# First mixture of an eight-expert layer: head statistics on VectorE and ScalarE, additions that leave sums, one of eight masked copies on GpSimd

## The reference, cut to what matters

```
y = scan output of the first branch                      # already computed, still unnormed
x = x + ga * (((y - mean(y)) * rsqrt(var(y) + eps)) * gamma + beta)
h = layernorm(x) * (1 + cb) + sb                         # per token, 128 features
sel = argmax(h @ gate_w + gate_b)                        # one expert of eight per token
x = x + gb * (h @ expert_w[sel] + expert_b[sel])
statistics of the new x                                  # for the next stage's layernorm
```

## Time and profile before

| what | us |
|---|---|
| median of 3 runs | 953.69 (953.1 to 953.91) |
| profiled execution: span, which is its own time here | 954.5 |
| TensorE busy in the span | 833.9 (87%) |
| VectorE busy | 776.2 (81%) |
| ScalarE busy | 656.3 (69%) |
| GpSimd busy | 568.8 (60%) |

### The profile page before, as it was taken

The page is one execution under the profiler, slowest core; times in us unless marked ns, Lnnn a source line. Parts: engine busy times, 40 slices in busy tenths (PEclk is TensorE's granted clock), DMA queues, the critical chain, the costliest instruction groups (busy, mean ns, idle before and its releaser), DMA issues.

```text
span 954.5 us, 23396 instructions
## 1 busy us (share of the span) xinstructions
PE 833.9 (87%) x7407; PEld 645.1 (68%) x7422; DVE 776.2 (81%) x2086; ACT 656.3 (69%) x1731; POOL 568.8 (60%) x571
## 2 busy tenths in 40 slices
PE   6969891699999957999999999999838999999990
PEld 5945471354445426888888888888617889999980
DVE  3988787889998858678999999999886866666996
ACT  3567126899996356567777877766456888888880
POOL 1211006757875143533688888888877777766773
PEclk9999796599999978999999999999858999999996
DMA  5330261322323203000011111111117666766987
GB/s 153 94 94 1 69 199 59 104 101 106 145 90 110 113 11 82 1 2 10 24 38 39 40 38 35 39 35 44 44 46 214 209 207 185 219 191 187 347 251 247
DMA packets 83461, 100.78 MB, mean 106 GB/s; under 512 B 15326, under 2 KB 65305, under 8 KB 81164
## 3 DMA queue, kind: packets, MB, share of 16 engines
q1 hardware_dynamic: 71388, 79.61, 27.3%
q0 software_dynamic: 8640, 17.97, 5.3%
q10 hardware_dynamic: 3312, 1.70, 0.6%
HBM read 75.71 MB, written 23.54 MB: 104 GB/s over the span
## 4 chain that ended last, share of the span: by engine, by line
PE 54%; DVE 4%; issue 2%; DMA 1%; SPq 1%; ACT 1%; POOL 0%; ACTq 0%; DVEq 0%
PE ps L2608 13%; PE ps L2365 12%; PE ps L2631 7%; PE ps L2381 3%; PE ps L2443 2%; PE ps L2356 2%; PE ps L2591 2%; PE ps L2327 2%; PE ps L2376 2%; PE ps L2502 2%; PE ps L2482 2%; PE ps L2342 1%; PE ps L2430 1%; PE ps L2626 1%; PE ps L2455 1%
## 5 line engine op out<-in xcount | busy, mean ns | idle before, releaser
L1551 POOL TENSOR_TENSOR kvb<-qk,v 128x1024 f32<-128x1024 f32 x64 | 126.2, 1976 | 74.6 <-DVE qk L1922 50.4
L1560 POOL DMA_INDIRECT rows_of<-payb,posu x128 | 144.7, 1131 | 40.7 <-issue 26.7
L1115 PE MATMUL ps<-masked,ew 128*128 128x512 f32 x256 | 129.9, 622 | 4.2 <-DVE masked L1043 3.5
L2365 PE MATMUL ps<-con,kvb 128*128 128x128 f32 x1024 | 126.0, 276 | 0.0
L2365 PEld LDWEIGHTS ps<-con,kvb 128*128 128x128 f32 x1024 | 119.4, 192 | 1.0 <-issue 1.0
L2287 DVE TENSOR_SCALAR qk<-ps,b 128x256 f32<-128x256 f32 x142 | 62.1, 479 | 47.7 <-PE ps L2608 43.2
L1043 DVE TENSOR_TENSOR masked<-f_t,wide 128x512 f32<-128x512 f32 x128 | 88.7, 711 | 9.6 <-PE ps L1115 9.3
L1584 POOL DMA_INDIRECT parts<-h,dest x72 | 76.9, 1068 | 26.6 <-issue 20.4
L1898 DVE TENSOR_TENSOR qc<-ps,qk 128x1024 f32<-128x1024 f32 x64 | 78.1, 1220 | 18.0 <-PE ps L2365 17.4
L1584 POOL DMA_INDIRECT parts<-gx,dest x70 | 75.4, 1077 | 25.5 <-issue 20.0
L1115 PEld LDWEIGHTS ps<-masked,ew 128*128 128x128 f32 x256 | 43.3, 193 | 47.2 <-issue 23.6
(11 more groups left out here) (367 smaller groups left out, 2130.4 us busy)
## 6 DMA issues: line engine op xcount, KB each, us to landing
wide<-hot_dram SPq DMA_DIRECT2D x16, 1024.0 KB, 4.6
kvb<-rows_of SPq DMA_DIRECT2D x71, 132.0 KB, 2.7
ex<-in_w_dram SPq DMA_DIRECT2D x36, 256.0 KB
lg<-in_w_dram SPq DMA_DIRECT2D x35, 256.0 KB
toep<-taps_dram SPq DMA_DIRECT2D x16, 512.0 KB, 5.8
xg<-parts SPq DMA_DIRECT2D x16, 512.0 KB, 5.5
x_tok<-in_x_dram SPq DMA_DIRECT2D x16, 256.0 KB, 3.0
rows<-rows_dram SPq DMA_DIRECT2D x16, 192.0 KB, 3.2
```

The costliest lines, as they stand in the source:

```text
L1115: nc.tensor.matmul(ps[:, w % 2, :], ew0[:, e, :], masked[e % 4][:, :], start=False, stop=(e == E - 1)).then_inc(s["product"], 1)
L1551: nc.gpsimd.tensor_tensor(kv[g % KB][:, :, :].rearrange("p e (h d) -> p e h d", h=H), k_in, v_in, ALU.mult).then_inc(s["kv"], 1)
L1560: nc.gpsimd.indirect_dma_start(rows_of, bass.IndirectOffsetOnAxis(ap=posu[w % PR][:, slot, t:t + 1], axis=0), pay[w % PB][:, t, :], None). ...
L2365: last = nc.tensor.matmul(cum(g)[:, e, :], kv[g % KB][:, e, :], k("upto"), start=True, stop=True)
```

## The change

VectorE and ScalarE make the statistics of the first four sequences alone: `statistics` for y for all sixteen, for x of sequences 0 to 3 `stats_x` (bn_stats and bn_aggr), the inverse root on ScalarE as Ln and Exp (`root_y`, `root_x`, with a table set loaded once), and `shift_x_head` on VectorE. For these sequences gamma is applied to (y - mean) in four pieces and the scale in `joined`, also four pieces. For sequences 4 to 15 `joined`, and for all sixteen `added`, are four scalar_tensor_tensor operations with a sum output in place of one addition and one reduction. `squares_y`, `sum_features`, `sum_x1` and `sum_x2` are gone. Mask 5 of every sequence and `bias_pieces` move to GpSimd. All five lists are written anew. The core of the diff:

```diff
-            moments = sb("moments", [P, 6 * C, 2], scope=sc)
+            moments = sb("moments", [P, TILES, 2], scope=sc)
+            HEAD = 4
...
+            BY_POOL = 5
             def expert(eng, name, w, e):
                 w, e = w + e // E, e % E
-                if exists(w):
+                if exists(w) and name == "masked":
+                    if e == BY_POOL:
+                        eng.wait_ge(s["masked_pool"], w + 1)
+                    else:
+                        eng.wait_ge(s["masked"], w * (E - 1) + e + (e < BY_POOL))
+                elif exists(w):
                     eng.wait_ge(s[name], w * E + e + 1)
...
-                    load_ahead(0)
-                    load_ahead(1)
-                    for w in range(B):
-                        load_ahead(w + 2)
-                        kept(w)
-                        spread(w)
+                    load_ahead(0); load_ahead(1); load_ahead(2); kept(0); spread(0); load_ahead(3); kept(1); spread(1); load_ahead(4)
+                    kept(2); spread(2); kept(3); spread(3); load_ahead(5); load_ahead(6); kept(4); spread(4); load_ahead(7); kept(5)
...
+                    def mask(w, e):
+                        landed(pool, s_wide, w)
+                        done(pool, "feat", w)
+                        expert(pool, "product", w, e - 4)
+                        nc.gpsimd.tensor_tensor(masked[e % 4][:, :], f_t[w % W][:, :], wide[w % W][:, e, :], ALU.mult).then_inc(s["masked_pool"], 1)
+
+                    nc.gpsimd.memset(eps[:, :], EPS).then_inc(s["eps"], 1)
+                    nc.gpsimd.tensor_scalar(down[:, :], k("iota"), -1.0, float(E), ALU.mult, ALU.add).then_inc(s["down"], 1)
+                    beta(0); beta(1); bias_pieces(); beta(2); beta(3); beta(4); beta(5); beta(6); beta(7); moments_mean(4); moments_scale(4)
+                    mask(0, 5); mean_x(4); mask(1, 5); beta(8); mean_2(0); scale_x(4); scale_2(0); moments_mean(5); moments_scale(5)
+                    moments_mean(6); moments_scale(6); moments_mean(7); moments_scale(7); moments_mean(8); moments_scale(8); mask(2, 5)
...
+                    def root(w, found, source, rs, logged, made):
+                        done(act, found, w)
+                        if w == 0:
+                            act.wait_ge(s["eps"], 1)
+                        nc.scalar.activation(tiles(rs, w), source[:, w * C:(w + 1) * C, 1], ACT.Ln, bias=eps[:, :]).then_inc(s[logged], 1)
+                        done(act, logged, w)
+                        nc.scalar.activation(tiles(rs, w), tiles(rs, w), ACT.Exp, scale=-0.5).then_inc(s[made], 1)
...
+                    nc.scalar.preload_act_table_set("natural_log_exp_and_others")
+                    root_y(0); root_y(1); root_x(0); norm_x(0); root_x(1); feat(0); root_y(2); norm_x(1); feat(1); hot_half(0); root_x(2)
...
+                    def stats_x(w):
+                        done(dve, "joined", w)
+                        done(dve, "stats_x", w - 1)
+                        for c in range(C):
+                            last = nc.vector.bn_stats(halves_x[:, c, :], x_tok[:, w * C + c, :])
+                        last.then_inc(s["sum_x"], 1)
+                        done(dve, "sum_x", w)
+                        for c in range(C):
+                            last = nc.vector.bn_aggr(moments_x[:, w * C + c, :], halves_x[:, c, :])
+                        last.then_inc(s["stats_x"], 1)
...
                     def gamma(w):
-                        if exists(w):
+                        if w < HEAD:
...
+                                last = nc.vector.scalar_tensor_tensor(yn[w % 2][:, c, :], features_of(t), moments[:, t, 0:1], rows[w % W][:, 0, :], ALU.subtract, ALU.mult)
...
-                            nc.vector.tensor_tensor(tiles(x_tok, w), tiles(x_tok, w), yn[w % 2][:, :, :], ALU.add).then_inc(s["joined"], 1)
...
+                                for c in range(C):
+                                    t = w * C + c
+                                    last = nc.vector.scalar_tensor_tensor(x_tok[:, t, :], yn[w % 2][:, c, :], rs_y[:, t:t + 1], x_tok[:, t, :], ALU.mult, ALU.add)
+                            else:
+                                for c in range(C):
+                                    t = w * C + c
+                                    last = nc.vector.scalar_tensor_tensor(x_tok[:, t, :], x_tok[:, t, :], 1.0, yn[w % 2][:, c, :], ALU.mult, ALU.add,
+                                                                          accum_out=sum_x[:, t:t + 1])
+                            last.then_inc(s["joined"], 1)
...
-                            nc.vector.tensor_tensor(tiles(x_tok, w), tiles(x_tok, w), ps[:, BACK, :].rearrange("p (c d) -> p c d", c=C), ALU.add).then_inc(s["added"], 1)
-
-                    def sum_x2(w):
-                        if exists(w):
-                            done(dve, "added", w)
-                            nc.vector.tensor_reduce(tiles(sum_2, w), tiles(x_tok, w), AX.X, ALU.add, negate=True).then_inc(s["sum2"], 1)
+                            for c in range(C):
+                                t = w * C + c
+                                last = nc.vector.scalar_tensor_tensor(x_tok[:, t, :], x_tok[:, t, :], 1.0, ps[:, BACK, c * D:(c + 1) * D], ALU.mult, ALU.add,
+                                                                      accum_out=sum_2[:, t:t + 1])
+                            last.then_inc(s["added"], 1)
...
+                    statistics(0); statistics(1); gamma(0); joined(0); stats_x(0); gamma(1); shift_x_head(0); joined(1); stats_x(1)
+                    statistics(2); shift_x_head(1); gamma(2); joined(2); best(0); stats_x(2); statistics(3); shift_x_head(2); best(1)
+                    gamma(3); joined(3); stats_x(3); statistics(4); shift_x_head(3); mask(0, 0); mask(0, 1); mask(0, 2); mask(0, 3)
+                    mask(0, 4); best(2); mask(0, 6); mask(0, 7); mask(1, 0); mask(1, 1); gamma(4); mask(1, 2); mask(1, 3); joined(4)
+                    mask(1, 4); statistics(5); added(0); mask(1, 6); mask(1, 7); statistics(6); statistics(7); best(3); statistics(8)
...
+                    mask(5, 3); mask(5, 4); gamma(9); joined(9); added(4); best(7); mask(5, 6); mask(5, 7); mask(6, 0); gamma(10)
+                    mask(6, 1); mask(6, 2); joined(10); mask(6, 3); statistics(11); mask(6, 4); added(5); best(8); mask(6, 6); mask(6, 7)
```

More of the change, by code:

```diff
@@ L746, in build @@
             TURN, BACK, LOGIT, HOT = 2, 3, 4, 5
-            names = ("weights", "split", "y_mean", "x_mean", "mean2", "y_sum", "y_sq", "y_ve", "y_rs", "y_shift", "y_normed", "gamma", "beta", "joined",
-                     "x_sum", "x_sq", "x_ve", "x_rs", "x_shift", "normed", "turned", "feat", "lg_ps", "equal", "down", "lg", "max", "idx", "idf", "hot",
-                     "hot_ps", "hot_b", "masked", "product", "moe_t", "moe_ps", "added", "sum2", "sq2", "ve2", "rs2", "shift2")
+            names = ("weights", "split", "eps", "y_mean", "x_mean", "mean2", "y_sum", "y_sq", "y_ve", "y_rs", "y_shift", "y_normed", "gamma", "beta", "joined",
+                     "log_y", "root_y", "sum_x", "stats_x", "log_x", "root_x", "shift_x", "x_sq", "x_ve", "x_rs", "x_shift", "normed", "turned", "feat", "lg_ps", "equal",
+                     "down", "lg", "max", "idx", "idf", "hot", "hot_ps", "hot_b", "masked", "masked_pool", "product", "moe_t", "moe_ps", "added", "sq2", "ve2", "rs2", "shift2")
+            from_tail = ("y_mean", "y_ve", "y_rs", "y_shift", "y_normed", "x_mean", "x_sq", "x_ve", "x_rs", "x_shift")
             s = {nm: sem(f"moe_{nm}") for nm in names}
@@ L1055, in _ @@
-                    sum_features(11); mask(5, 1); gamma(10); mask(5, 2); sum_x2(3); mask(5, 3); best(7); mask(5, 4); joined(10)
-                    mask(5, 5); added(4); mask(5, 6); sum_x1(10); mask(5, 7); mask(6, 0); sum_features(12); mask(6, 1); gamma(11)
-                    mask(6, 2); sum_x2(4); mask(6, 3); best(8); mask(6, 4); joined(11); mask(6, 5); added(5); mask(6, 6); sum_x1(11)
-                    mask(6, 7); mask(7, 0); sum_features(13); mask(7, 1); gamma(12); mask(7, 2); sum_x2(5); mask(7, 3); best(9)
@@ L1059, in _ @@
-                    mask(7, 4); joined(12); mask(7, 5); added(6); mask(7, 6); sum_x1(12); mask(7, 7); mask(8, 0); sum_features(14)
-                    mask(8, 1); gamma(13); mask(8, 2); sum_x2(6); mask(8, 3); best(10); mask(8, 4); joined(13); mask(8, 5); added(7)
-                    mask(8, 6); sum_x1(13); mask(8, 7); mask(9, 0); sum_features(15); mask(9, 1); gamma(14); mask(9, 2); sum_x2(7)
-                    mask(9, 3); best(11); mask(9, 4); joined(14); mask(9, 5); added(8); mask(9, 6); sum_x1(14); mask(9, 7); mask(10, 0)
@@ new lines, in _ @@
+                    mask(1, 4); statistics(5); added(0); mask(1, 6); mask(1, 7); statistics(6); statistics(7); best(3); statistics(8)
+                    mask(2, 0); mask(2, 1); mask(2, 2); mask(2, 3); mask(2, 4); added(1); gamma(5); mask(2, 6); joined(5); best(4)
```

(15 more changed lines are left out.)

212 lines of the change are left out of this document (99 added, 113 removed).

## The result

| | us | ratio to the kernel before, 95% interval |
|---|---|---|
| kernel before, median of 20 runs | 953.8 | |
| changed kernel, median of 20 runs | 956.49 (952.71 to 961.75) | 1.0029 [1.0016, 1.0042] |
| changed kernel, second series (12 runs; before 953.63) | 956.16 | 1.0022 [1.0001, 1.0042] |
| changed kernel, third series (12 runs; before 953.29) | 956.65 | 1.0037 [1.0017, 1.0056] |

The change makes the kernel slower by 0.2 to 0.4%. Forecast were 950.7 us and 0.48 for faster; the time lies inside the range, on the other side. The profiled execution of the changed kernel was one of its fastest: 953.03 us for a span of 951.2. A time is thus 1.8 us above its span, so the profile of before (span 954.5) shows an execution of about 956.3 and not, as I had taken it, one 0.8 above the median.

A forecast was written before the change was run, and what follows sets the result against it. VectorE and ScalarE were taken to set the stage's pace, TensorE having some 0.7 us to spare a sequence. Head -6.5, A +4.9, B -0.6 and tail -0.8 summed to -3.0 us, so 950.7 us, range 941 to 961.

The forecast's parts named there:

- Head: Stage start, from VectorE's first instruction to mask(0, 0): first mask at 176.5 in place of 183.0, -6.5 us.
- The wide copy: Head: the copy that mask(0, 0) needs lands at 174.9 us, before that mask starts at 176.5.
- A: Sequences 0 to 3, mask(0, 0) to mask(4, 0): from 40.8 to 45.7 us, +4.9.
- the locks: GpSimd's masks and betas holding VectorE's two-tile operations: 3.0 us in A, 4.2 us in B.
- VectorE's waits: VectorE waiting for the slow TensorE at the start: 2.5 us kept in A.
- rival 4: GpSimd's queue is late and TensorE waits for mask(2, 5); 4 us late gives 955 us; chance 0.06.
- The sum-leaving additions: VectorE's joined and added in four pieces: 0.27 us each, 1.08 in place of 1.21 per join or addition.
- B: Sequences 4 to 11, mask(4, 0) to mask(12, 0): from 80.9 to 80.3 us, -0.6.
- Rest: Tail from mask(12, 0): stays TensorE's; less TensorE backlog and the last sum's own wait give -0.8 us.
- Rival 1: VectorE falls below TensorE, which sets the pace: A 40.6, B 76.8, in all -11.6, 942 us; chance 0.27.
- Rival 2: GpSimd's sixth masks hold VectorE at full price: 965 us, half-way 958; decides above 0.51 us mean price; chance 0.20.

The follow-up runs named there:

- second and third: Profiles of the changed kernel run again unaltered, against the kernel before: 1.0022 [1.0001, 1.0042] and 1.0037 [1.0017, 1.0056].
- third profile of before: Profile of the kernel before, unaltered, in its second repeat: one run, 951.09 us, stage 200.76 us.

## Why the prediction was wrong, step by step

**Head: -6.5 forecast, -5.0 measured.** At the end of statistics(2) VectorE was 0.7 us behind my times. Then an operation that I had at nothing, `shift_x_head(1)` on 128x4 elements, stood under the row of four betas. GpSimd, then VectorE:

```profile
156.75 4.93 POOL L875 TENSOR_TENSOR x_tok<-x_tok,rows 128x512 f32<-128x512 f32 x4
```

```profile
159.33 2.37 DVE L1026 SCALAR_TENSOR_TENSOR stat<-moments_x,stat 128x4 f32<-128x4 f32 x1
161.63 1.43 DVE L1034 SCALAR_TENSOR_TENSOR yn<-xg,moments,rows 128x128 f32<-128x128 f32 x4
```

It ended when the last beta did. gamma(2), which I had between two betas, came behind them and ran free (1.43). The two together took 3.7 us where I had 3.5 for gamma(2) alone, so this hold, which I had not seen, is only 0.2 of the 1.5 us missed; the run that held the betas back gained only 0.4. The other 0.6 us were lost over the rest of the list. The wide copy was in time, as forecast: the first mask waited for VectorE's own list.

**A: +4.9 forecast, +4.0 in the first trace, +5.5 in the second and third.** The sum came out near, in part by luck. Against the run without GpSimd's long operations (VectorE busy 38.04 in A) the locks are 3.7 to 4.3 us, where I had 3.0; VectorE's waits are 1.5 to 3.5, where I had 2.5; its own work, gaps included, is the 39.1 that are left, where I had 40.2. What I had only as a rival is TensorE's wait for mask(2, 5): rival 4, given 0.06, with its place named rightly. TensorE stands idle for 2.1 to 2.7 us there, and A is 1.5 us longer where the wait is the longer one and the clock falls.

**The sum-leaving additions: 0.27 forecast, 0.21 measured.** This was off in the change's favour: VectorE's work in B is then 8 x 8 x 0.06 = 3.8 us less, 72.3 and not 76.1.

**B: -0.6 forecast, +1.0 to +1.9 measured (up to +2.4 against the third profile of before). This is the step that failed.** I took B as VectorE's work of eight sequences plus what GpSimd's locks add, 76.1 + 4.2, with no term for waits of VectorE: I read VectorE's 79.97 of 82.70 us as its being the limit all along, and let every sequence shrink as its work did. But the eight are not alike. All six `statistics` of B stand in VectorE's list ahead of mask(10, 0). The stretches up to that mask and behind it, and VectorE's waits in the first:

```profile
219.91:282.99 63.08, 57.26 (x222) 29.21 (x223) 60.67 (x229) 53.65 (x168) 56.04 (x85) 1.00 0.31 110
282.99:301.86 18.87, 18.87 (x75) 9.94 (x74) 15.84 (x61) 16.72 (x58) 13.86 (x24) 1.00 0.29 112
```

```profile
DVE logit L1060 <- PE ps L1130: 0.9, 1, 0.9
```

For six sequences VectorE is the limit: it waits 0.9 us in 63, the rest of its idle time being gaps between instructions, while TensorE is idle for 5.8. For the last two TensorE is the limit: it is busy 18.87 of 18.87 us, and VectorE waits 2.4 us for it. By taking the mean of VectorE's work over all eight I counted its relief in the last two as a gain, though TensorE's floor lies there. The terms as measured: VectorE's own work with its gaps 73.6 (72.3 by my prices, with the additions at 0.21), locks 5.05 (4.2), waits 3.3 (none), together 81.95.

The locks are the difference of VectorE's busy time to the run without long GpSimd operations. That run's B is shorter by the same 5.0 us, all of it ahead of mask(10, 0) (58.08 in place of 63.08, then 18.88), and VectorE idles as long in it. Had a late queue of GpSimd made the difference, VectorE would have lost it waiting.

TensorE's waits in the changed kernel, from the first mask to 302 us (us in total, times, longest):

```profile
PE ps L1138 <- DVE hot L1072: 5.8, 6, 2.0
PE ps L1158 <- DVE masked L1090: 2.4, 2, 1.4
PE ps L1158 <- POOL masked L897: 2.1, 1, 2.1
PE ps L1130 <- ACT f_t L966: 1.7, 2, 1.2
```

Before, the same view has one line, 3.5 us for the first masks. The largest group is the transposes of the choice waiting for `best`; without GpSimd's long operations it is 1.0 us. Two holds make its longest wait. GpSimd, VectorE and TensorE:

```profile
234.10 1.21 POOL L897 TENSOR_TENSOR masked<-f_t,wide 128x512 f32<-128x512 f32 x1
...
237.33 2.50 POOL L875 TENSOR_TENSOR x_tok<-x_tok,rows 128x512 f32<-128x512 f32 x2
```

```profile
234.23 1.24 DVE L1053 SCALAR_TENSOR_TENSOR x_tok<-x_tok,yn 128x128 f32<-128x128 f32 x1
...
237.34 1.36 DVE L1072 TENSOR_TENSOR hot<-down,lowest 128x96 f32<-128x96 f32 x1
```

```profile
238.85 0.60 PE L1138 MATMUL ps<-con,hot 128*24 128x128 f32 x4 [1.95 <-DVE hot L1072]
```

The hold of `joined` (0.96 us) and of `hot` (1.10) come to 2.06 us, about the 1.95 that TensorE waits. I had priced holds by what they do to long masks; they also fall on the 128x32 and 128x96 operations of the choice, which TensorE waits for at once. Not every wait of the group has such a hold: ahead of the one of 1.15 us at 249.24 no operation of the choice was held, and VectorE only came to it late, without having waited. TensorE's own 9.6 us a sequence, which I had summed, is what sequences 10 to 13 measure (9.5).

**Rest: -0.8 forecast, -0.1 measured.** This part is TensorE's. That a TensorE with less backlog would shorten it was only argued, and did not come.

Together, against the first profile of before: -5.0 + 5.5 + 1.0 - 0.1 = +1.4 in the second trace, +2.3 in the third, and about 0 in the first, against -3.0. The other 1 to 2 us between the medians aren't placed: the stretch behind the stage varied by 3.4 us among profiles (604.4 to 607.8), with no kernel always longer.

**Rivals.** Rival 1 (942) is near what the kernel does with GpSimd's long operations gone, 945.1. Its floor for B was right (76.8 forecast, 76.96 measured), that for A was not (40.6, 42.94); the way there is closed by the locks. Rival 2 was on the measured side for another reason than its own: the masks cost 0.2 us each, below its 0.51. Rival 4 is part of the cause. Undoing it alone moved the wait by one sequence.

## What to carry to other kernels

Where two engines are near each other in work per sequence, don't take the mean over many sequences. Look where in the list the work stands, sum each engine by stretch, and take the longer one each time: here VectorE was the limit for six sequences and TensorE for two, and a relief counts only where its engine is the limit. Price GpSimd's two-tile operations by the short operations of VectorE that they may fall on, not only by the long ones. Before a forecast is made of a written-out order, follow the queue of the engine that nobody calls the bound: a mask moved to GpSimd cost 2.3% in the kernel before, where it stood behind chains that waited for ScalarE, and nothing clear in the changed one. No run tried another place for it in the kernel before.

## What the hardware showed that was not expected

- A row of GpSimd operations keeps VectorE's short one waiting through more than one of them: 2.37 us for 128x4 elements, whose own time is 0.13, until the row of four betas ended. It goes the other way as well. In the second trace a row of five VectorE masks (the first row) holds a 128x4 operation of GpSimd (the second) until its end; in the first trace the same one, at the same point of the row, took 0.46. GpSimd starts its next chain 1.9 us later for it, but mask(2, 5) only 0.3 us, since in the first trace other operations were held. The Trainium skill, SBUF — State Buffer, "Who interferes with whom", calls the port pair that VectorE and GpSimd share "an exclusive lock", which a VectorE instruction with two SBUF inputs and a GpSimd instruction that reads SBUF contend for. These rows agree, and show the one engine held through several instructions of the other.

```profile
196.45 3.07 DVE L1090 TENSOR_TENSOR masked<-f_t,wide 128x512 f32<-128x512 f32 x5
```

```profile
197.31 2.26 POOL L858 TENSOR_TENSOR stat<-stat,stat 128x4 f32<-128x4 f32 x1
```

- Reading the sum of a 128x128 addition (80 ns) costs nothing: the step is 0.21 us with one source in PSUM and with both in SBUF.
- At one place an idle time of TensorE of 2.14 us left the granted clock at 1.00 and one of 2.74 us was followed by a stretch of 0.66 to 0.70, in two of three executions of one kernel. At another place an idle time of 1.15 us was followed by such a stretch in one of three. So the idle time alone doesn't tell whether the clock falls.
